# The query, key and value projection from three float32r products, row loads of 16 rows, and the feed-forward weights prepared one stage earlier

## The reference, cut to what matters

```
x:  (2, 4096, 256) float32;  W_qkv: (256, 768);  16 heads of 16
xn = (x - mean(x)) / sqrt(var(x) + 1e-5)                      # over the last axis
q, k, v = split(xn @ W_qkv + b_qkv)                           # per head
attn = softmax(q k^T) v                                       # 4096 x 4096 per head, not scaled
h = xn @ W_exp + b_exp                                        # 256 -> 1024
h = gelu(butterfly(h, up_weights) + up_bias)                  # exact gelu
y = butterfly(h, down_weights) @ W_con + b_con + down_bias    # 1024 -> 256
out = x + attn + y
```

## Time and profile before

| | us |
|---|---|
| median of 3 runs | 5649.99 |
| the profiled execution, its own time | 5647.46 |
| its span | 5645.7 |
| stage 1 ends, first score product of stage 2 | 223.94 |
| last superblock to the last sum | about 5187 to 5261 |
| first product of stage 3 | 5280.10 |

### The profile page before, as it was taken

The page is one execution under the profiler, slowest core; times in us unless marked ns, Lnnn a source line. Parts: engine busy times, 40 slices in busy tenths (PEclk is TensorE's granted clock), DMA queues, the critical chain, the costliest instruction groups (busy, mean ns, idle before and its releaser), DMA issues. The chain is left out here.

```text
span 5645.7 us, 97311 instructions
## 1 busy us (share of the span) xinstructions
PE 5595.4 (99%) x35876; PEld 2607.8 (46%) x35876; DVE 4886.6 (87%) x9104; ACT 4972.7 (88%) x9648; POOL 524.8 (9%) x482
## 2 busy tenths in 40 slices
PE   8899999999999999999999999999999999999999
PEld 5444444444444444444444444444444444444698
DVE  6699999999999999999999999999999999997333
ACT  3599999999999999999999999999999999999544
POOL 2246553000000000000000000000000000000000
PEclk9899999999999999999999999999999999999999
DMA  8611121000000000000000000000000000000111
GB/s 288 210 35 51 51 58 34 17 21 21 20 14 15 21 21 21 21 15 21 21 21 17 12 20 21 21 21 18 18 21 21 19 14 16 21 21 2 34 45 41
DMA packets 232761, 197.02 MB, mean 35 GB/s; under 512 B 171752, under 2 KB 192616, under 8 KB 220520
## 3 DMA queue, kind: packets, MB, share of 16 engines
q1 hardware_dynamic: 228848, 168.00, 10.5%
q0 software_dynamic: 3456, 23.07, 1.4%
HBM read 128.07 MB, written 60.82 MB: 33 GB/s over the span
## 5 line engine op out<-in xcount | busy, mean ns | idle before, releaser
L654 ACT ACTIVATE probs<-psum 128x512 f32<-128x512 f32 x8192 | 4222.5, 608 | 292.2 <-PE psum L845 290.3
L708 DVE TENSOR_REDUCE maxima<-psum 128x1 f32<-128x512 f32 x6042 | 3970.9, 686 | 358.0 <-PE psum L823 252.3
L823 PE MATMUL psum<-k_rows,q_rows 48*128 48x512 f32 x7049 | 2494.2, 454 | 0.6 <-ACT spill L670 0.6
L859 PE MATMUL psum<-probs,v_cols 128*32 128x512 f32 x16384 | 2183.3, 605 | 0.0
L845 PE MATMUL psum<-q_rows,k_rows 50*128 50x512 f32 x8192 | 2054.1, 423 | 0.0
L823 PEld LDWEIGHTS psum<-k_rows,q_rows 48*128 48x128 f32 x7049 | 1176.2, 184 | 1246.9 <-DVE maxima L704 812.0
L845 PEld LDWEIGHTS psum<-q_rows,k_rows 50*128 50x128 f32 x8192 | 1263.7, 185 | 129.8 <-ACT probs L654 40.1
L704 DVE CUSTOM_DVE_ANT_0 merged<-psum,spill 128x512 bf16<-128x512 f32 x1007 | 685.9, 681 | 2.7 <-issue 1.9
L670 ACT ACTIVATE spill<-psum 128x512 f32<-128x512 f32 x1007 | 601.3, 597 | 16.5 <-PE psum L823 16.0
L859 PEld LDWEIGHTS psum<-probs,v_cols 128*32 128x32 f32 x16384 | 322.5, 108 | 619.1 <-issue 324.0
L823 PEld LDWEIGHTS psum<-k_diff,q_rows 48*128 48x128 f32 x1007 | 184.4, 183 | 845.2 <-DVE maxima L708 790.3
(11 more groups left out here) (96 smaller groups left out, 2027.4 us busy)
## 6 DMA issues: line engine op xcount, KB each, us to landing
q_rows<-q_parts SPq DMA_DIRECT2D x128, 256.0 KB
q_parts<-parts SPq DMA_DIRECT2D x32, 512.0 KB, 6.1
k_parts<-parts SPq DMA_DIRECT2D x32, 512.0 KB, 4.5
k_rows<-k_parts SPq DMA_DIRECT2D x64, 256.0 KB
q_rows<-q_parts SPq DMA_DIRECT2D x128, 128.0 KB
planes<-in_up_planes POOLq DMA_DIRECT2D x10, 1024.0 KB, 10.6
planes<-in_down_planes POOLq DMA_DIRECT2D x10, 1024.0 KB, 5.0
y<-in_x SPq DMA_DIRECT2D x16, 512.0 KB, 5.7
```

The costliest lines, as they stand in the source:

```text
L654: nc.scalar.activation(probs[:, 2 * (u % 2) + half, BANK * g:BANK * g + BANK], ps_s[:, r % 4, :], ACT.Exp).then_inc(s_exp, 1)
L708: nc.vector.tensor_reduce(largest, region(use), axis=AX_X, op=ALU.max).then_inc(s_region_free, 1)
L823: nc.tensor.matmul(region(use_of[n, j]), q_rows[m % 4][lower:lower + ROWS, P * t:P * t + P], keys[lower:lower + ROWS, :], start=True, stop ...
L859: last = nc.tensor.matmul(ps_o[VW * g:VW * g + VW, :], v_cols[:, KT * (head % 2) + UNITS * half + at, :], probs[:, 2 * (u % 2) + half, BAN ...
```

## The change

What the change does:

- q, k and v come from three float32r products (high x high, low weights x high xn, high weights x low xn) instead of one float32 product. W_qkv is split once (ACT high, DVE low). Per chunk ACT makes `xt_high` from PSUM beside the copy `xnt`, DVE makes `xt_low`.
- The normalisation moves from DVE to ACT: DVE only makes `nbias` = -mean/std, ACT computes xn from x with scale and bias.
- v is stored by chunk, 4 KB in a row for each partition, instead of by head in rows of 256 bytes; a head's v is then loaded by 8 transfers instead of one.
- Every load of query and key rows names 16 rows; before, a load of 32 rows (two copies or two parts of 16) and one of 16 stood side by side. 6 instead of 4 loads for a superblock's queries, 9 instead of 6 for a head's keys.
- The transposes, splits and bias of the feed-forward weights move from the start of stage 3 into the last superblock of stage 2, one output tile per unit, into buffers that this superblock no longer uses.

```diff
         def load_q(sp, head, half, slot, halves=(0, 1)):
             rows = bass.ds(HD * head, HD)
             for lower in (HALF_P * n for n in halves):
-                for first, part, copies in ((0, 0, 2), (2, 1, 1)):
-                    src = q_dram[part:part + 1, rows, QB * half:QB * half + QB].to_broadcast([copies, HD, QB])
-                    dst = q_rows[slot][lower + HD * first:lower + HD * (first + copies), :].bitcast(F32)
+                for first, part in enumerate((0, 0, 1)):
+                    src = q_dram[part, rows, QB * half:QB * half + QB]
+                    dst = q_rows[slot][lower + HD * first:lower + HD * first + HD, :].bitcast(F32)
                     sp.dma_start(dst, src).then_inc(s_q[slot], 16)
...
-                    dst = v_dram[bass.ds(HEADS * b, HEADS), :, bass.ds(CT * of_row, CT), :].rearrange("h p t d -> p h (t d)")
-                    sp.dma_start(dst, v_sb[:, HEADS * p:HEADS * p + HEADS, :]).then_inc(s_v_out[p], 16)
+                    sp.dma_start(v_dram[c, :, :, :], v_sb[:, p, :, :]).then_inc(s_v_out[p], 16)
...
+                def normalise(c, p):                       # ACT
+                    act.wait_ge(s_nbias, c + 1)
+                    if c > 1:
+                        act.wait_ge(s_xt_ps, c - 1)
+                    for t in range(CT):
+                        nc.scalar.activation(xn[:, CT * p + t, :], x_tile(c, t), ACT.Identity, bias=nbias[:, p, t:t + 1],
+                                             scale=rstd[:, p, t:t + 1]).then_inc(s_xn, 1)
+                def copy_turned(c, q):                     # ACT
+                    act.wait_ge(s_xt_ps, c + 1)
+                    if c > 1:
+                        act.wait_ge(s_v_ps, 2 * (c - 1))
+                        act.wait_ge(s_xt_out[q], 16 * (c // 2))
+                    for k in range(KD):
+                        nc.scalar.copy(xt_high[:, KD * q + k, :], ps_xt[:, k, :]).then_inc(s_xt_high, 1)
+                        nc.scalar.copy(xnt[:, KD * q + k, :], ps_xt[:, k, :]).then_inc(s_xt, 1)
...
+                def low_turned(c, q):                      # DVE
+                    if c > 1:
+                        dve.wait_ge(s_v_ps, 2 * (c - 1))
+                    for k in range(KD):
+                        dve.wait_ge(s_xt, KD * c + k + 1)
+                        nc.vector.tensor_tensor(xt_low[:, KD * q + k, :], ps_xt[:, k, :], xt_high[:, KD * q + k, :].bitcast(F32),
+                                                ALU.subtract).then_inc(s_xt_low, 1)
...
                     for m in range(KD):
                         low_part(c, m)
                     if left > 2:
-                        normalise(c + 2, p)
+                        scale_mean(c + 2, p)
+                    if left > 1:
+                        low_turned(c + 1, 1 - p)
...
+                    passes = [(w, x, k) for k in range(KD)
+                              for w, x in ((wqkv_high, xt_high), (wqkv_low, xt_high), (wqkv_high, xt_low))]
                     for m in range(2 * KD):
                         if m == KD and left > 1:
                             transposes(c + 1, 1 - p)
-                        for k in range(KD):
-                            last = nc.tensor.matmul(ps_qk[:, m, :], wqkv[:, k, P * m:P * m + P],
-                                                    xnt[:, KD * p + k, :], start=(k == 0), stop=(k == KD - 1))
+                        for n, (w, x, k) in enumerate(passes):
+                            last = nc.tensor.matmul(ps_qk[:, m, :], w[:, k, P * m:P * m + P], x[:, KD * p + k, :],
+                                                    start=(n == 0), stop=(n == len(passes) - 1))
...
+                    if LAST <= u < LAST + HT:              # PE, stage 2, after the unit's sums
+                        turn_weights(u - LAST)
+                    if u == LAST + HT + 1:
+                        turn_bias()
```

## The result

The changed kernel takes 5619.26 us (median of 4 runs, 5615.97 to 5620.07), the kernel before 5650.65 beside it: ratio 0.9941, 95% interval 0.9929 to 0.9953, or -31.4 us on the medians. The forecast was 5619. The total fell where it was put, but four of its terms did not, nor did one stretch that had no term; they cancelled.

A forecast was written before the change was run, and what follows sets the result against it. In the projection, PE products (7.8 us) plus an ACT-DVE chain (4.17) bound each 12.0 us chunk, DMA close behind. Projection -25.2, last superblock +1.0 and feed-forward start -6.9 sum to -31.1: 5619 us, range 5608 to 5640.

The forecast's parts named there:

- slow chunks 10 to 14: Projection chunks behind the row loads: 53.7 us instead of 71.2 with 16-row loads, -17.5 us.
- the last chunk: Last projection chunk: 12.7 us instead of 15.7 from cheaper wide products and no low clock, -3.0 us.
- the feed-forward stage's start: Start of the feed-forward stage: weight work gone, SP's load comes first, first product earlier, -6.9 us (bounds -5.5 to -7.5).
- A: Rival, projection: PE's clock falls in every chunk, eleven more chunks lose 1.7 us, +18.7, total 5638; chance 0.13.
- B: Rival, projection: no gain in the chunk, from handoffs or v's store; +14 us, total 5633; chance 0.17.
- C: Rival, projection: row loads still stand in one place, +7.6 to +11 us, total 5627 to 5630; chance 0.08.
- D: Rival, projection: PE stays at 1.2 GHz throughout, a chunk takes 16.5 us, +86, total 5705; chance 0.04.
- Start: Before the first q/k product: W_qkv's rounding and extra conversions stand ahead on ACT and DVE, +3.9 us (bounds +3 to +6).
- Chunks 0 to 9: First ten projection chunks: each 1.2 us shorter, -12.0; with the clock loss of +3.4, -8.6 us.
- the clock term: Projection chunks 7 and 8: PE waits 2.5 us and drops to 1.2 GHz, 1.7 us lost each, +3.4 us.
- Transfers in attention: Attention: about ten more SP transfers after each head, nothing waiting behind them for half a superblock, 0 us.
- Last superblock: End of attention: two transposes a unit hidden in PE's 0.22 us spare, bias-row lump outruns slack, +1.0 us (0 to 3.5).

The follow-up runs named there:

- rows16: Kernel before with only the q, k and k-difference row loads as one 16-partition transfer per part instead of 32 and 16; 5642.04 us, ratio 0.9978.
- v_by_head: Changed kernel with v stored again by head in 256-byte runs and loaded by one transfer a head; 5623.06 us, ratio 0.9951 to the kernel before.

## Why the prediction came out right, and where it was wrong

**Right by its mechanism.** The slow chunks 10 to 14 (-16.1 for -17.5; chunk 13's low clock alone is 1.6), their cause (rows16), the last chunk (-3.1 for -3.0), three products and the shorter chain in a chunk (10.6 for 10.8, with a wait of 1.1 for 1.3), the feed-forward stage's start (-7.1 for -6.9). None of the rivals happened: the clock did not fall in every chunk (A), the gain in the chunk was there (B), 16-row loads cost next to nothing (C), and in the projection, once at 2.4 GHz, PE left it only behind two waits, of 2.3 and 2.0 us (D). Of the signs two were missed: ScalarE waited up to 3.1 us for stored parts where no wait over 2 was to be, and the last superblock ended 8.2 us later, not 1. The DMA share near 1 that was to be a sign of being wrong came (0.99), without a wait of ScalarE for stores in those chunks.

One reading of the prediction goes further than its rows: that the old loads stood on two engines because they have 32 rows. Their outermost dimension of two fits the same rows, and the edit took both away.

**Start (+3.9, measured +8.1).** The instructions were counted rightly (+4.4 with GpSimd held), and +6.3 to +8.1 is what seven traces with this start have. The step that failed is the price: VectorE's rounding of W_qkv was priced as if alone. I asked what each engine had to do, not what stood beside it; GpSimd's addition was in the old kernel already.

**Chunks 0 to 9 (-8.6 with the clock, measured -13.3).** The term was too small in three places: the first chunk alone is 2.7 us shorter (12.1 for 14.8), the period is 0.2 shorter, and the clock term (+3.4) was half, one fall of 1.6 instead of two. The DMA sums had two faults that did no harm. A chunk's demand with the new v was put at 9.4 us, 0.87 of the chunk, and the share was 0.99; with the old v it was put at 11.2, and v_by_head kept 10.6 us in four of five chunks at a share of 1.01. So v's short runs were priced at 1.75 us of DMA time a chunk and show 0.3.

**Transfers in attention (0, measured +4.5 once).** "Nothing waits behind them" was right of SP's queue. What failed was to ask only what the change adds: everything behind the projection moved by 24 to 26 us except one load, which hangs on GpSimd's chain and moved by 36, and so met the row.

**Last superblock (+1.0, bounds 0 to 3.5, measured +8.2).** The step "0.22 hidden to the last" failed. PE's free time in a unit was not free at that place: two transposes behind the last sums cost 0.37 a unit, eight times (3.0). And the bias row as a lump of 1.94 cost, beside itself, the clock: three groups of sums at half pace with the scores between them, the 3.3 us that are left of the 8.2. The rows of before showed the clock low only behind waits of 1.9 us and more; here it fell behind 1.94 us of one-column products without a wait, and with these spread or moved away it stayed at 1.00.

**Feed-forward pace (0, measured -7.8).** No term stood for it. The new addresses of the weights take part in it: moving them alone made the kernel before 2 to 14 us faster. How, and what decides between the two faster paces, is open.

The errors are +4.2, -4.7, +1.4, -0.1, +3.75, +7.2, -0.2 and -7.8: together +3.7. The forecast of the total owes its exactness to that, which is luck, and to where the profiled runs lie: the one before 3.2 us below the median of its runs, the one after 0.8 above, so that 27.4 us in the traces are 31.4 on the medians.

## What to carry to other kernels

When work is moved, list what every other engine does at that moment, unchanged work included: the three new costs here (GpSimd beside VectorE, a planes load beside a small row, a lump of tiny products between full ones) came from what stood beside what, not from the length of what was added. Free time on an engine that takes turns with another is not free at every place: the same two transposes made a unit of 4.14 us one of 4.43, 4.51 or 4.68 at three places. Try the place before crediting the gap. And where a view shows a load standing on few DMA engines beside stores, try another shape of it first: here that was 12.9 us for a change of a few lines.

## What the runs showed of the hardware

- A 128x768 float32 subtraction with both inputs in SBUF took 0.9 us on VectorE alone and, two in a row, 2.0 to 2.9 each beside GpSimd additions from SBUF, the more when GpSimd began first.
- 16 products of one column each, 1.94 us, were followed by the granted clock at 0.50 for the stretch 5227 to 5233; spread two at a time between scores they left it at 1.00 (5220 to 5240).
- A single 50x512 score between two 128x128 transposes took 0.43 us, four in a run 0.66.
- Row loads of 16 rows, the rows outermost, left the chunks behind them at 11.3 to 12.65 us, where those with loads of two times 16 rows took 13.4 to 17.6 (rows16).
- The same feed-forward code ran with down products of 283, 281 or 276 ns, constant over a whole run. The placement of buffers takes part between the first and the others; what decides between the last two is open.
- Two 16 KB transfers issued 0.8 us ahead of a 1 MB load on another queue let PE go on 7.9 us after their issue, 3.9 of them a wait; issued 2.2 us ahead of it they kept nobody waiting (rows16, v_by_head).
